# Moving outputs, turns, logits and query copies inside four attentions

## The reference

```
h = tok(x)
h = h + L0_attn(layernorm(h)); h = h + L0_ffn(layernorm(h))   # rope, causal; 8 experts, top 1
h = h + L1_attn(layernorm(h)); h = h + L1_ffn(layernorm(h))   # grid attention; gated attention
h = h + L2_attn(layernorm(h)); h = h + L2_ffn(layernorm(h))   # second layer norm inside; 8 experts top 2 and a shared one
h = h + L3_attn(layernorm(h)); h = h + L3_ffn(layernorm(h))   # band mask; 16 experts, top 8
```

## Time and profile before

| what | value |
| --- | --- |
| median of 3 runs | 732.2 us (731.81 to 741.64) |
| profiled execution | 738.21 us, its span 736.5 us |
| mean granted TensorE clock | 0.963 |
| TensorE busy | 95% of the span |
| TensorE weight loads | 86% |
| VectorE busy | 68% |
| ScalarE busy | 48% |
| GpSimd busy | 23% |
| DMA | 39.40 MB, mean 54 GB/s |

### The profile page before, as it was taken

The page is one execution under the profiler, slowest core; times in us unless marked ns, Lnnn a source line. Parts: engine busy times, 40 slices in busy tenths (PEclk is TensorE's granted clock), DMA queues, the critical chain, the costliest instruction groups (busy, mean ns, idle before and its releaser), DMA issues.

```text
span 736.5 us, 16233 instructions
## 1 busy us (share of the span) xinstructions
PE 696.1 (95%) x6345; PEld 629.9 (86%) x6345; DVE 500.9 (68%) x1240; ACT 351.5 (48%) x809; POOL 167.1 (23%) x164
## 2 busy tenths in 40 slices
PE   6999999999999999999998999999999999999996
PEld 6788898999988777798877998889999967779995
DVE  3658468888877952878565783577766768556785
ACT  0367355555543232678443442455544445247663
POOL 1200026544351122334022000035443220000000
PEclk9999899999999998999798998999999999699999
DMA  9922022222221000002200010022231200112100
GB/s 250 270 69 81 2 58 79 80 80 79 65 68 58 1 0 1 3 2 74 58 1 1 2 45 2 31 73 60 71 107 28 85 1 2 52 42 80 32 23 24
DMA packets 16283, 39.40 MB, mean 54 GB/s; under 512 B 3596, under 2 KB 4588, under 8 KB 15759
## 3 DMA queue, kind: packets, MB, share of 16 engines
q1 hardware_dynamic: 14232, 37.29, 17.7%
q10 hardware_dynamic: 1976, 1.08, 0.6%
HBM read 37.90 MB, written 0.44 MB: 52 GB/s over the span
## 4 chain that ended last, share of the span: by engine, by line
PE 74%; DVE 15%; issue 4%; ACT 4%; POOL 2%; DMA 1%; POOLq 0%; ACTq 0%; DVEq 0%; SPq 0%
PE PS L720 7%; PE PS L849 6%; PE PS L793 5%; PE PS L601 4%; PE PS L605 4%; PE PS L603 4%; PE PS L604 4%; PE PS L602 4%; PE PS L729 4%; PE PS L814 3%; PE PS L653 3%; DVE AL L1571 2%; PE PS L839 2%; PE PS L656 2%; PE PS L655 2%
## 5 line engine op out<-in xcount | busy, mean ns | idle before, releaser
L1034 ACT ACTIVATE MIX<-PS 128x288 f32<-128x288 f32 x118 | 48.4, 411 | 116.7 <-PE PS L605 116.4
L601 PE MATMUL PS<-XH,WH 128*128 128x288 f32 x284 | 86.7, 305 | 3.4 <-DVE OT L1560 1.4
L1893 POOL TENSOR_TENSOR rstd<-var,nhalf 96x3 f32<-96x3 f32 x18 | 17.9, 992 | 295.3 <-DVE var L1307 295.3
L603 PE MATMUL PS<-XH,WL 128*128 128x288 f32 x284 | 83.9, 295 | 0.0
L602 PE MATMUL PS<-XL,WH 128*128 128x288 f32 x284 | 83.8, 295 | 0.0
L604 PE MATMUL PS<-X,WH 128*128 128x288 f32 x284 | 83.7, 295 | 0.0
L605 PE MATMUL PS<-X,WL 128*128 128x288 f32 x284 | 83.6, 294 | 0.0
L1560 DVE TENSOR_TENSOR OT<-MIX,PS 128x288 f32<-128x288 f32 x94 | 42.2, 450 | 39.0 <-ACT MIX L1034 38.4
L1571 DVE TENSOR_TENSOR AL<-OT,AH 128x288 fp32r<-128x288 f32 x118 | 58.9, 507 | 3.3 <-ACT AH L1048 2.3
L1414 DVE TENSOR_TENSOR WL<-RG,WH 128x768 fp32r<-128x768 f32 (+2 forms) x46 | 57.8, 1258 | 3.5 <-ACT WH L1014 3.3
L653 PE MATMUL PS<-AH,DW 128*128 128x288 f32 x166 | 52.3, 315 | 7.2 <-DVE AL L1571 7.0
(11 more groups left out here) (256 smaller groups left out, 1737.8 us busy)
## 6 DMA issues: line engine op xcount, KB each, us to landing
RG<-in_gu_l0f_dram SPq DMA_DIRECT2D x8, 512.0 KB, 4.5
RG<-in_gu_l0f_dram SPq DMA_DIRECT2D x16, 256.0 KB, 5.7
RG<-in_gu_l2f_dram SPq DMA_DIRECT2D x9, 384.0 KB, 3.6
RG<-in_gu_l2f_dram SPq DMA_DIRECT2D x18, 192.0 KB, 4.3
RD<-in_wd_l0f_dram SPq DMA_DIRECT2D x8, 384.0 KB, 3.2
RD<-in_wd_l2f_dram SPq DMA_DIRECT2D x9, 288.0 KB, 2.8
RD<-in_wd_l3f_dram SPq DMA_DIRECT2D x6, 384.0 KB, 3.1
BIG<-in_patch_dram SPq DMA_DIRECT2D x6, 288.0 KB, 8.3
```

The source lines that it names most:

```text
L601: mm(o, WH[r][:, 0, w], XH[:, cols], start=True, stop=False)
L603: mm(o, WL[r][:, 0, w], XH[:, cols], start=False, stop=False)
```

## The change

- Outputs of half 0. In A0 and A3 all three tiles stand in the pass after the last `qk`, right behind the last `scores`. In A1 and A2 (`wide`) tile 0 comes two passes, tile 1 one pass before that, both behind the pass's scores, and tile 2 ahead of the last scores. VectorE's parts of the next norm move a pass ahead; in A1 and A2 the norm of the probabilities goes ahead of them and `shift` behind part 0.
- Half 1 of A2 is turned in pass 3 and copied out in pass 4; its values come in passes 5 to 7, through banks 2 and 3. The parts of its norm stand in VectorE's passes 0, 1 and 2. The first mix waits until the turned half has been copied out, and the mixes wait for half 1's values only at unit 6.
- `gate_logits` comes in four portions behind values 4 to 7; `router_exp` moves to pass 1 on ScalarE.
- A2's weights are loaded in three portions (nine DMAs for three), the value columns after A1's last values, the others after its ninth and twelfth `token_major`; the splitting copies move with them into A1's passes.
- A3's queries are copied by ScalarE, by `activation` with a scale per partition, where VectorE did it by `tensor_scalar`.

```diff
 def pieces(a, i):
     n = 4 if a.tm else 3
+    i -= 4 if a is A2 else 0
...
+def value_bank(a, j, p):
+    return (2 if a is A2 and j else 4 + 2 * j) + p % 2
...
-W2 = [(0, 1536, 2304), (1, 1536, 2304), (0, 0, 768), (1, 0, 768), (0, 768, 1536), (1, 768, 1536)]
+W2 = [(0, 1536, 2304), (1, 1536, 2304), (1, 0, 768), (0, 0, 768), (0, 768, 1536), (1, 768, 1536)]
...
-    return {A0: 3, A1: 4, A2: 7, A3: 3}[a]
+    return {A0: 3, A1: 4, A2: None, A3: 3}[a]
@@ SP @@
-            qkv(A2)
+            second_weights(0, A2.v0, A2.width)
+            for n in range(2):
+                sp.wait_ge(S["tm_ready"], TM0["l1f"] + 9 + 3 * n)
+                second_weights(1 + n, 768 * n, 768 * (n + 1))
@@ TensorE, qk, A2 @@
+                            if u == 0 and k == 0:
+                                pe.wait_ge(S["y_taken"], TAKEN[stage])
@@ TensorE, mix @@
+                    if u == (a.ng if a is A2 else 0):
+                        pe.wait_ge(S["v_sb"], V0[a.name] + 2 * a.vpieces)
                     if u == 0:
-                        pe.wait_ge(S["v_sb"], V0[a.name] + 2 * a.vpieces)
+                        wait_xv(a, 1)
@@ TensorE, the passes @@
-                            if a.gated and p == 6:
-                                gate_logits()
                             values(0, p)
+                            if a.gated and p >= 4:
+                                last = gate_logits((2 * p - 8, 2 * p - 7))
+                                if p == 7:
+                                    last.then_inc(S["logits"], 1)
+                    if a is A2 and i == 3:
+                        turn(stage, 1)
                     for p in pieces(a, i):
                         values(1, p)
                     if 0 <= i - lag < a.units:
                         qk(i - lag)
+                    n = i - lag - a.units
+                    if wide and n == 0:
+                        output(range(2, TAU), range(a.ng)).then_inc(S["y_ready"], 1)
                     if 0 <= i - lag - 1 < a.units:
                         scores(i - lag - 1)
+                    if n == (-2 if wide else 0):
+                        pe.wait_ge(S["o_sb"], u0 + a.ng)
+                        pe.wait_ge(S["v_sb"], V0[a.name] + 2 * a.vpieces)
...
+                        last = output(range(1 if wide else TAU), range(a.ng))
+                        if not wide:
+                            last.then_inc(S["y_ready"], 1)
+                    if wide and n == -1:
+                        output(range(1, 2), range(a.ng))
...
-                    if i == a.first_out:
...
-                        output(range(1), range(a.ng))
-                    if i == a.first_out + 1:
-                        output(range(1, TAU), range(a.ng)).then_inc(S["y_ready"], 1)
@@ ScalarE, the passes @@
+                    if a is A2 and i == 4:
+                        x2_high(stage, 1)
                     for p in pieces(a, i):
                         vals(1, p)
+                    if a.gated and i == 1:
+                        router_exp(1, HB * GRP, 128)
                     if 0 <= i - lag < a.units:
                         keys(i - lag)
-                        if a.tm:
+                        if a is not A2:
                             queries(i - lag)
...
-                    if a is A1 and i >= a.units + lag + 1:
-                        for n in range(2):
-                            w2_split(2 * (i - a.units - lag - 1) + n)
+                    if a is A1 and i in (8, 9, 11, 13, 15, 16):
+                        w2_split((8, 9, 11, 13, 15, 16).index(i))
@@ VectorE, second_half_in @@
-                for part in range(3):
-                    layer_norm(k, 1, (part,))
-                    if a is A2 and part < 2:
-                        w2_split(2 + part)
+                if a is A2:
+                    return
+                layer_norm(k, 1)
@@ VectorE, the passes @@
+                lag, wide = a.lag, a.ng == 6
                 for i in range(a.units + lag + 4):
+                    if a is A2 and i == 0:
+                        layer_norm(stage, 1, (0,))
+                    if a is A2 and i == 4:
+                        evac_xt(stage, "attn", a, 1)
...
-                    if not a.tm and 0 <= i - lag < a.units:
+                    if a is A2 and 0 <= i - lag < a.units:
                         queries(i - lag)
+                    tail = wide and i >= a.units + lag
+                    if tail and 0 <= i - lag - 2 < a.units:
+                        norm(i - lag - 2)
+                    part = i - lag - a.units - (0 if wide else 1)
+                    if wide and 0 <= part < 3:
+                        if a is A1 and part == 2:
+                            w2_split(3)
+                        layer_norm(stage + 1, 0, (part,))
                     if 0 <= i - lag - 1 < a.units:
                         shift(i - lag - 1)
...
-                    if 0 <= i - lag - 2 < a.units:
+                    if not tail and 0 <= i - lag - 2 < a.units:
                         norm(i - lag - 2)
...
-                    part = i - a.first_out - 2
-                    if a is A1 and part >= 1:
-                        w2_split(part - 1)
-                    if 0 <= part < 3:
+                    if not wide and 0 <= part < 3:
                         layer_norm(stage + 1, 0, (part,))
-                    if a is A2 and i == 0:
-                        for n in range(4, 6):
-                            w2_split(n)
+                    if a is A1 and i in (9, 10, 12):
+                        w2_split((9, 10, 12).index(i))
+                    if a is A2 and i in (1, 2):
+                        layer_norm(stage, 1, (i,))
+                    if a is A2 and i < 2:
+                        w2_split(4 + i)
```

More of the change, by code:

```diff
@@ L395, in bass_vit_tower @@
         in_att = {n: sem("in_att_" + n) for n in ("l0a", "grid", "l1f", "l2a", "l3a")}
+        in_w2 = [sem(f"in_w2_{k}") for k in range(3)]
         in_patch = [sem(f"in_patch{k}") for k in range(TOKF)]
@@ L460, in qkv, with second_weights @@
             def qkv(a):
[L461 to L465, removed]
                 for c in range(NC_):
                     sp.dma_start(wqkv[a.name][0:CB[c], c, :], t[f"wqkv_{a.name}_{c}"]).then_inc(in_att[a.name], 16)
+            def second_weights(n, lo, hi):
+                sp.dma_start(wqkv["l2a"][:, 0, lo:hi], t["wqkv_l2a_0"][:, lo:hi]).then_inc(in_w2[n], 16)
+                for half in (0, 64):
+                    sp.dma_start(wqkv["l2a"][half:half + 64, 1, lo:hi], t["wqkv_l2a_1"][0:64, lo:hi]).then_inc(in_w2[n], 16)
             def proj(a):
@@ L698, in attention, with gate_logits @@
                 W, P2 = wqkv[a.name], wp[a.name]
-                def gate_logits():
-                    wait_xv(a, 1)
-                    for i in range(HB):
+                def gate_logits(pairs):
+                    if 4 in pairs:
+                        wait_xv(a, 1)
+                    for i in pairs:
                         for c in range(NC_):
@@ L705, in gate_logits @@
                                       wr[1][0:CB[c], c, :], start=(c == 0), stop=(c == NC_ - 1))
-                    last.then_inc(S["logits"], 1)
+                    return last
                 def token_major(u):
@@ L1153, in queries @@
                             rows = VW + a.fq
-                            o = QB[u % 2][0:rows, 0:HB // 2, h * N:(h + 1) * N].rearrange("f i (m t) -> f t i m", t=TAU)
-                            last = activation(o, PS[0:rows, 0, 0:HN // 2].rearrange("f (t i m) -> f t i m", t=TAU, m=NB), ACT.Copy,
-                                              scale=mh[0:rows, h:h + 1])
+                            o, i = QB[u % 2][0:rows, 0:HB // 2, h * N:(h + 1) * N], PS[0:rows, 0, 0:HN // 2]
+                            if a.tm:
+                                o, i = o.rearrange("f i (m t) -> f t i m", t=TAU), i.rearrange("f (t i m) -> f t i m", t=TAU, m=NB)
+                            else:
+                                i = i.rearrange("f (i n) -> f i n", n=N)
+                            last = activation(o, i, ACT.Copy, scale=mh[0:rows, h:h + 1])
                     last.then_inc(S["q_sb"], 1)
@@ L1722, in queries @@
                         dve.wait_ge(S["s_ready"], U - 1)
-                    rows = VW + a.fq
-                    for h in range(a.hg if a.paired else 0):
-                        last = V.tensor_scalar(QB[u % 2][0:rows, 0:HB // 2, h * N:(h + 1) * N],
-                                               PS[0:rows, 0, 0:HN // 2].rearrange("f (i n) -> f i n", n=N),
-                                               mh[0:rows, h:h + 1], None, ALU.mult)
-                    for h in range(0 if a.paired else a.hg):
+                    for h in range(a.hg):
                         o, i = q_views(a, u, h)
@@ L1789, in attention @@
                         down_low(a.then, 0)
-                    part = i - a.first_out - 2
-                    if a is A1 and part >= 1:
```

(10 more changed lines are left out.)

36 lines of the change are left out of this document (17 added, 19 removed).

## The result

The change makes the kernel 0.6% faster: 732.7 us against 737.9 us, medians of 20 runs each, ratio 0.9936 with a 95% interval of 0.991 to 0.9963. The direction and the range of the forecast held.

A forecast was written before the change was run, and what follows sets the result against it. TensorE, busy 95% of the span, was taken as bound, losing 27.5 us to slow clock. Base 732.2, waits +2.2, clock -11.3 (14.5 times 0.78) gave 723.1, say 724 us; range 714 to 738.

The forecast's parts named there:

- the stall: Before layer 2's half 1 turn: TensorE waits about six us, new waits net +5.9; as deciding rival 738 us, chance 0.18.
- stretches four and five: Slow-clock stretches following waits of 1.8 and 2.3 us at the turns into layer 2; not among those that can go.
- layer 3: Query copies move from VectorE to ScalarE at 0.9 us a unit; waits change by -1.3 us.
- the logits: Layer 1's gate logits spread between values: same TensorE time, whole gain is slow stretch two, 3.5 us.
- Stretch seven: Slow-clock stretch in layer 3, loss 6.8 us; half counted as gone, 3.4.
- layer 1's last units: Wide matmuls fill passes of the 10.2 us slow stretch, half counted gone, 2.6 us; turn into layer 2 -0.5.
- layer 2's end: The norm TensorE waited 1.24 us for comes a pass earlier: -1.2 us.
- stretch six: Slow-clock stretch at layer 2's end, counted as gone whole, 3.3 us.
- layer 0's end: Outputs in one block let the layer norm start 2 us sooner; the turn's 0.72 us wait goes, -0.7.
- no stall: Rival at layer 2's half 1: VectorE reaches the norm's parts early, 5.9 + 1.3 us fall away, 717 us; chance 0.12.
- five named slow stretches: Stretches one, two, three, six and seven, 22 us that can go; rival that all go: 719 us, chance 0.15.
- ScalarE did not become layer 3's bound: Rival in layer 3: products wait about 0.8 us more in six units, stretch seven stays, 731 us; chance 0.05.

The follow-up runs named there:

- Experiment 3: The changed kernel with ScalarE's copies of turned probabilities and mix ahead of the last exponential in layers 1 and 2's last units: 728.5 us.
- experiment 6: The changed kernel with half 0's outputs, the norm's parts and VectorE's tail order back in their old places: 739.1 us.
- 10: Old half 1 of layer 2, VectorE's last passes in order norm, shift, part, and ScalarE's copies before the last exponential, else the changed kernel: 718.7 us.
- 5: The changed kernel with layer 2's half 1 as before the change: 722.1 us.
- 11: The changed kernel with old half 1, order norm, shift, part, and two weight splits back between the parts of half 1's norm: 720.7 us.
- 4: The changed kernel with half 1's norm in layer 2 whole, ahead of the queries of unit 0: 724.5 us.
- 7: The changed kernel with layer 2's half 1 as before and VectorE's order norm, shift, part in layers 1 and 2's last passes: 719.1 us.
- experiment 9: The changed kernel with old half 1, order norm, shift, part, and the gate logits in one block again: 721.8 us.

## Why the forecast was right and wrong

**Right: the stall itself.** Forecast: 21.5 us from the first value to the turn of half 1, 7.1 of them waiting. Measured: 393.55 - 372.95 = 20.6 us, and 5.25 + 1.04 = 6.3 of waiting, ended by the last part of the norm. The 1.6 before mix 0 were hidden by the low clock; 1.0 came at two of the passes with moved values, for ScalarE (414.50 and 421.21), which the sum did not have. That layer 2's waits add up to the forecast's +4.7 is partly luck: the missed 1.0 at its end stands against the 1.6 that were hidden. The clock term of layer 2's start, 1.7 us, was also right: one stretch of 13.8 us at 0.51 loses 6.8, stretches four and five lost 5.1.

**Right, with luck: layer 3 and the logits.** Three query copies take 0.92 us on ScalarE against 0.9 forecast, ScalarE's own waits are 0.34, 0.59 and 0.80, together 1.7 against 1.5, and the 1.71 is gone; but 0.50 us before the outputs are new, so the section's idle time fell by 0.5 where 1.3 was forecast. Stretch seven went whole, where half was counted. That is luck of the profiled execution: of the eleven profiles with ScalarE's query copies six have a slow stretch in layer 3, which loses 1.7 to 3.4 us. The logits gave 3.4 of 3.5.

**Wrong: layer 1's last units and layer 2's end.** This is the step that failed in the mechanism, and behind it the clock term. The forecast costed the moved norm part as a length in VectorE's chain ("10.4 us ... against 9.0 before") and said that at layer 2's end the wait of 1.24 goes. It followed who waits for VectorE's shift only one step, to the exponential, and not to what is queued behind that exponential on ScalarE. There stood the copy of the turned probabilities, for which TensorE waits: 2.19 us in layer 1, 1.07 in layer 2, where 0 was forecast in both. Against the forecast that is 0.9 us of idle time in layer 1's section. Experiment 3, which moves only ScalarE's copies, takes both waits away, and 4.2 us by the medians.

The larger part of the miss is clock: stretch six was counted as gone whole and three by half, but slow stretches of 3.6 us at layer 2's end and of 3.5 and 3.4 us in layer 1's last units stayed. That is 1.7 us of busy time in layer 2's section and 1.3 in layer 1's. Whether the new waits cause these stretches is open. Leaving out experiment 6, whose outputs are not moved, in layer 1 all four profiles with a wait of 1.4 to 2.2 us for PT or PN have the stretch of 361.4, and so have two of the seven with 1.0 or none. At layer 2's end it stands in experiments 3 and 10, where the wait is gone, and not in 5 and 11, where 1.07 and 1.01 us are left.

**Wrong: the base.** The forecast took the median of three, 732.2, for the kernel and the profiled 738.2 for an execution with 6 us too much slow clock, and so scaled its clock gains by 0.78. In 20 runs the kernel before has a median of 737.9, and of 738.6 to 740.5 in the three later sets. The profiled execution was the typical one. The clock gave back 13.6 us where the unscaled terms had 14.5; the factor was wrong. The forecast time, 724, misses the measured 732.7 by 8.7 us: 5.7 are the base; the sections gave 5.0 less than the unscaled -12.3; the medians fell by 2.1 less than the two profiled spans did; and the factor and the rounding took back 3.2 and 0.9.

**Mis-sized: layer 0's end, and what came after.** The wait of 0.72 went and one of 0.49 for ScalarE's copy before the outputs came (76.16), so that -0.1 is left of -0.7, and 2.7 of the 3.4 of clock arrived. After layer 3 a slow stretch of 4 us stands at 719, which no part of the change touches. Such a stretch is in six of the twelve profiles of changed kernels, within 703 to 723 us. Its cause is open: no run was made for it.

**The rivals.** The stall did not make the change a loss. Its price there was 5.9 + 3.4 = 9.3 us, and experiments 4, 5 and 7 put it at 8 to 11. The forecast itself counted 5.9 + 1.7 = 7.6, against the half 1 of the kernel before; under the rest of the change the old half 1 would have waited 1.8 us less and kept its clock. With no stall 717 was forecast, on a base 5.7 us too low; the kernels without one take 719 to 725. Three of the five named slow stretches went whole, not all five, and ScalarE did not become layer 3's bound: its waits there are the 1.7 us above. The Trainium skill (TensorE: Matmul & The Clock Gate, "Loop structure matters more than you think"), which the forecast cited for the clock, names waiting between matmuls as what puts it low. The 13.8 us stretch around the wait of 5.25 agrees; the one at the logits block of experiment 9 has no wait ahead, and those of layer 2's end do not follow the wait for PT.

## What to carry to other kernels

When an instruction is moved ahead of another on an in-order engine, follow the delayed one through every queue: its reader on the next engine delays whatever stands behind it there, and that may be the copy for which the bounding engine waits. Count a slow stretch as gone only after several profiles: which stretches one execution shows differs from kernel to kernel where the waits are nearly the same. Price each part of a change against the kernel as the other parts leave it, not against the kernel before; here the moved half was put at 7.6 us and cost 8 to 11. And take the base from enough runs: a profiled execution above a median of three is as likely to be the typical one.

## What the runs showed of the hardware

GpSimd's power on 96x3 elements takes 0.85 us alone and 1.49 us when VectorE's split of 768 columns, with two SBUF inputs, has started 0.17 us before it. That split ends at 372.61 and the power at 373.32 (371.83 + 1.49), 0.71 after it. The Trainium skill (SBUF — State Buffer, "SBUF: two separate sides") says that a VectorE operation with two SBUF inputs and a GpSimd operation that reads SBUF exclude each other from a shared port pair for the whole instruction. The rows agree: the power lasts almost its full length past the end of the split.

Three query copies cost about as much on ScalarE as on VectorE (379 and 361 ns each), so moving them pays only by whose queue is free.
